# A strip of zeros of 320 numbers in place of 448 behind each gather of a graph network

## What is computed

```
h = relu(layernorm(x))                       # 12500 x 128
q, k, v = h @ Wq.T, h @ Wk.T, h @ Wv.T       # 8 heads of 16
s  = (q[dst] * k[src]).sum / 4 + edge_attr @ We.T
a  = exp(s - segment_max(s, dst)) / segment_sum(...)
x  = x + segment_sum(v[src] * a, dst)
h  = relu(layernorm(x))
for W, b, g, beta in three layers:           # relu in the first two
    h = segment_sum((h @ W)[src] * norm, dst) + b
    h = batch_norm(h) * g + beta
out = x + h
```

## Time and profile before

| | us |
|---|---|
| median of three runs | 6214.33 |
| the profiled execution, its time | 6205.67 |
| the profiled execution, its span | 6203.9 |
| PE busy in the span | 5259.4 (85%) |
| DVE busy | 4526.3 (73%) |
| POOL busy | 4496.4 (72%) |
| ACT busy | 2295.7 (37%) |
| attend, from to | 220 to 2749 |
| aggregate, layers 1, 2, 3, from to (rounded) | 3550 to 4290, 4470 to 5230, 5400 to 6120 |

### The profile page before, as it was taken

One profiled execution on the slowest core, in us unless ns is written; L12 is line 12 of the kernel. 1 busy time (PEld: TensorE's weight loads), 2 busy tenths in 40 slices (PEclk: granted clock), 3 DMA queues, 4 the chain that ended last, 5 costly groups with the idle time before them and its releaser, 6 DMA issues. The chain is left out here.

```text
span 6203.9 us, 165021 instructions
## 1 busy us (share of the span) xinstructions
PE 5259.4 (85%) x49582; PEld 3541.0 (57%) x49582; DVE 4526.3 (73%) x13500; ACT 2295.7 (37%) x5686; POOL 4496.4 (72%) x6062
## 2 busy tenths in 40 slices
PE   3688888888888888874799699998899997699995
PEld 2355555555555555553577467675476765467674
DVE  7566666666666666668899688886488887788886
ACT  3333333333333333333344244443644443444442
POOL 2588888888888888867000198886298886588883
PEclk9655565555555655555677699999999999899997
DMA  4433333333333333324333443333433334533335
GB/s 134 137 100 99 100 99 99 99 99 100 99 98 100 99 99 99 99 80 134 110 92 95 122 117 112 112 117 99 136 113 114 114 112 106 179 112 114 114 111 163
DMA packets 542000, 688.39 MB, mean 111 GB/s; under 512 B 217072, under 2 KB 427905, under 8 KB 541722
## 3 DMA queue, kind: packets, MB, share of 16 engines
q0 software_dynamic: 140208, 338.71, 19.8%
q1 hardware_dynamic: 401692, 348.45, 18.8%
HBM read 619.25 MB, written 67.52 MB: 111 GB/s over the span
## 5 line engine op out<-in xcount | busy, mean ns | idle before, releaser
L730 POOL DMA_INDIRECT at_kv<-kv_tab,at_idx x1568 | 1541.5, 983 | 276.6 <-POOL at_rest L734 139.6
L2247 ACT ACTIVATE ag_msg<-ag_pair 128x768 bf16<-128x768 f32 x1200 | 944.2, 809 | 1371.1 <-PE ag_pair L2177 1298.5
L2186 PE MATMUL ag_sum<-ag_hot,ag_msg 128*128 128x240 bf16 x10800 | 1267.4, 267 | 1.1 <-DVE ag_msg L2116 0.7
L2186 PEld LDWEIGHTS ag_sum<-ag_hot,ag_msg 128*128 128x128 bf16 x10800 | 982.9, 98 | 334.0 <-issue 287.6
L2058 POOL DMA_INDIRECT ag_spill<-g_tab,ag_idx x600 | 587.2, 979 | 687.0 <-DMA ag_idx<-spill_tab 578.5
L2099 DVE TENSOR_SCALAR ag_hot<-iota_win,ag_node 128x240 bf16<-128x240 bf16 x4350 | 994.4, 339 | 0.0
L2067 POOL DMA_INDIRECT ag_spill<-g_tab,ag_idx x750 | 731.1, 975 | 126.3 <-POOL ag_rest L2070 80.9
L2177 PE MATMUL ag_pair<-xs,ag_pick 128*32 128x384 bf16 x14400 | 758.9, 330 | 67.3 <-issue 62.9
L734 POOL MEMSET at_rest<- 8x448 f32 x1568 | 723.2, 461 | 0.1
L2116 DVE CAST ag_msg<-ag_pair 128x768 bf16<-128x768 f32 x600 | 570.2, 950 | 131.5 <-PE ag_pair L2177 104.8
L2177 PEld LDWEIGHTS ag_pair<-xs,ag_pick 128*32 128x32 bf16 x14400 | 301.0, 96 | 330.0 <-issue 214.7
(11 more groups left out here) (333 smaller groups left out, 9313.9 us busy)
## 6 DMA issues: line engine op xcount, KB each, us to landing
ag_pick<-slot_tab SPq DMA_DIRECT2D x150, 768.0 KB
rk_hi_bc<-hi_tab SPq DMA_DIRECT2D x50, 896.0 KB
at_attr<-attr SPq DMA_DIRECT2D x196, 128.0 KB
at_qd<-q_tab SPq DMA_DIRECT2D x1568, 12.0 KB
at_kv<-kv_tab,at_idx POOLq DMA_INDIRECT x1568
ag_spill<-g_tab,ag_idx POOLq DMA_INDIRECT x1350
tr_dv<-dinv_tab SPq DMA_DIRECT2D x72, 256.0 KB
g_tab<-xs SPq DMA_DIRECT2D x48, 384.0 KB
```

Source lines behind the costliest of these rows:

```text
L730: nc.gpsimd.indirect_dma_start(kv[:, s.slot, ch, :], None, env["kv_tab"], bass.IndirectOffsetOnAxis(ap=idx[:, s.slot, ch:ch + 1], axis=0)) ...
L2186: last = nc.tensor.matmul(sum_ps[k][:, 0:WIN], row[:, part * DIM:(part + 1) * DIM], hot[:, k, ch, :], start=first and part == 0, stop=end ...
L2247: nc.scalar.activation(msg[:, p % 4, :, :], pair_ps[p % 3][:, :, 0:3 * DIM], ACT.Copy).then_inc(copied[p], 1)
```

## The change

One constant is smaller, so that each of the 1568 memsets of attend (L734) and each of the 1350 of the three aggregates (L2061, L2070) writes 8x320 numbers in place of 8x448. The instructions of every engine keep their number, their order and their waits.

```diff
-REST = 448
+REST = 320
```

## The result

In the comparison that the prediction was made for, the changed kernel took a median of 7122.66 us (four runs, 7109.76 to 7139.39) against 6213.55 of before (6210.10 to 6214.83): a ratio of 1.1468, 95% interval 1.1454 to 1.1482. Forecast were 6046 us, with a range up to 6130. The same changed kernel, run later on another chip beside the same kernel before, took 6039.44 us against 6212.68 (ratio 0.9723, interval 0.9692 to 0.9754). What stands between 7123 and 6039 is what the experiments had to find.

What follows compares the result with a forecast made beforehand. POOL was taken to bound attend and, by a little, the aggregates; savings of 118 us in attend and 50 in the aggregates gave 168, so 6038 from the profiled 6205.67, stated as 6046 us for the median, range 5985 to 6130.

Steps and rivals of the forecast that it cites:

- The memset: Strip memset after each gather in attend and the aggregates: 461 ns falls to 354 in attend, saving 107 ns each.
- clean distance: Attend: time from one gather to the next with nothing held, 1.573 us before, 1.466 us after the change.
- Attend, on a full chip: Attend, forecast for any chip: block falls from 12.91 to 12.31 us, saving 118 us over 196 blocks.
- The phase on which the forecast rests: Attend: L808 runs about 9.9 us after the last gather, so one gather start per block falls inside it.
- The held gathers: Attend: gathers starting within L808 are held, 0.45 us per block, mean of L730 rising from 983 to some 1010 ns.
- Rival A: Attend: nothing held more than now, the full 0.856 us per block saved, total 5996 us; chance 0.13.
- rival B: Attend: one gather per block held the full 1.08 us, only the aggregates' 50 us remain, 6164 us; chance 0.13.
- The wait of L767 for `at_kv`: Attend: DVE's wait for gathered rows before its product should shrink from 218.5 to some 100 us.
- The aggregates, on a full chip: Aggregates, forecast for any chip: POOL's gathers drop to 13.97 us, PE sets the round, saving 50 us, range 35 to 71.
- PE's own round: Aggregates: time between two L2217 with no idle time before the second, 14.49 us, taken as the new bound.
- DVE's own round: Attend: DVE's block without its wait for gathered rows, 12.91 less 1.11, taken as 11.80 us.
- Rival C: Attend: held time spreads to DVE's small two-input instructions, block 13.94 us, total 6366 us, slower; chance 0.07.

Runs made afterwards that it cites:

- e9: The changed kernel word for word, run again beside the kernel before on a chip with nearly complete semaphore-update records; 6039.44 us, ratio 0.9723.
- e11: The kernel before, unchanged, profiled on the same chip as e9; 6214.81 us.
- e8: Kernel before with the 320 strip in attend and no gathers from attend's fifth block on, rows of the first four reused; 5816.60 us.
- e16: The kernel of e8 once more, on a thin chip (many semaphore-update records missing); 5907.05 us, kernel before there 6308.11.
- e6: Kernel before, strip 448, with the eighth gather and its memset left out from attend's fifth block on; 5932.11 us.
- e12: The kernel of e6 once more, on a chip called thin by its records alone; 5943.81 us, kernel before there 6204.42.
- e5: Kernel before with only the memsets shortened to 320 in all stages, the tile staying at 448 so addresses stay; 6032.94 us.
- e1: Kernel before with the 320 strip in attend only, 448 in the aggregates; 6736.29 us, kernel before there 6305.62.
- e4: Kernel before with strip 256 in all stages; 7769.40 us, kernel before there 6305.62.
- e2: Kernel before with the 320 strip in the three aggregates only, 448 in attend; 7033.03 us, kernel before there 6305.62.
- e3: Kernel before with strip 384 in all stages; 7100.05 us, kernel before there 6305.62.
- e15: Kernel before with strip 320 in attend and, from the fifth block on, gathers fetching a quarter of the bytes in as many rows; thin chip, 6778.95 us.
- e14: Kernel before with strip 320 in attend and two more memsets per block to slow POOL again; thin chip, 6590.15 us, kernel before there 6201.17.

## Why the prediction was wrong, step by step

**The memset.** Forecast 354 ns and a clean distance of 1.466 us; measured 355 ns in after and 354 in e9, and 1.47 between gathers. Right.

**Attend, on a full chip.** The phase on which the forecast rests is there: from the last gather of a block to L808 are 9.9 us at the median, in e9 as in e11. Forecast 12.31 us per block and 118 us; e9 against e11 gives (2662.1 - 248.8) / 195 = 12.38 and (2768.8 - 250.7) / 195 = 12.91, that is 105 us. The ends of these sums are in the rows of L808 of e9 and e11:

```profile
L808 DVE TENSOR_TENSOR at_msg<-at_kv,at_msg x196: 1210/1219/1270, 248.8 to 2662.1; 128x1024 f32<-128x1024 f32 x196
```
```profile
L808 DVE TENSOR_TENSOR at_msg<-at_kv,at_msg x196: 1210/1218/1270, 250.7 to 2768.8; 128x1024 f32<-128x1024 f32 x196
```

**The held gathers.** Forecast a mean of 1010 ns for L730, 0.45 us held per block. The page of e9:

```profile
L730 POOL DMA_INDIRECT at_kv<-kv_tab,at_idx x1568 | 1602.9, 1022 | 277.6 <-POOL at_rest L734 188.5
```

That is 8 x 0.070 = 0.56 us, 0.11 more than forecast, and this term is what makes the block 12.38 and not 12.31. A smaller error of the sum: of the 0.33 us by which the block before is longer than the clean one it names 0.13 and 0.25, which are 0.38, so that the same terms counted on both sides would have saved 0.65 us per block and not 0.60. Rival A (nothing held any more than before) would have had 983 ns or less, and rival B some 1090. By the Trainium skill's page Perfetto Trace Analysis, section DMA Instruction — SWDGE (GPSIMD), such instructions do not read a tensor, by which none would be held at all; the traces do not agree, with a longest gather of 2.02 us in e9. The wait of L767 for `at_kv` fell from 229.4 us in e11 to 163.1 in e9, where I had said some 100.

**The aggregates, on a full chip.** Forecast 50 us. First to last L2217: 2547.1 us in e11 (3558.6 to 6105.7) and 2486.2 in e9 (3454.7 to 5940.9), 61 us. The spans of PE are 14.6 us, and its own round was put at 14.49. POOL waits for PE before L2067 now (24.1 us in e9), as forecast. The spans of the whole program, 6213.1 and 6045.0 us, differ by 168.1; the sum was 168. That it comes out to the microsecond is luck: attend gave 13 us less than forecast and the aggregates 11 more.

**The step that failed** is the one that no rival took up: "PE's own round is what lies between two L2217", and "DVE's own round would be about 1.1 us shorter". Both were taken as constants of the kernel. On a thin chip they are not: there PE's results come the later, and these rounds are the longer, the closer POOL's gathers stand. With them 1.47 us apart PE's results come 3 us late, DVE's round is 15.06 us instead of at most 11.80, and PE's in the aggregates over 18 instead of 14.49. The prediction said that it would fail "if PE's round in aggregate rises above 14.49", which it did, but it gave that no chance and no price. Rival C had the right sign with the wrong mechanism: it had gathers held by DVE, and in after hardly any is (mean 960 ns, where 952 is a gather that is not held).

**DVE's own round** was also too long in itself. Without gathers it is 10.90 us (e8) and 10.83 (e16), not 11.80: the 1.11 us of waiting for `at_kv` are not all that the gathers cost. With seven of the eight gathers the whole block is 11.50 (e6). Part of this may be PE's clock, whose granted value in attend (250 to 2200 us) is 0.68 in e8, 0.64 in e6 and 0.58 in before. The sum did not rest on it.

**Could the trace of before have told?** It had two signs. The landing times were missing from its list of DMA issues (though e12 shows that a thin trace can have them), and in 100 of the 196 blocks DVE's wait before L786 was put down to "issue", where e11 names PE nearly always:

```profile
DVE at_ml L786 <- issue: 111.3, 100, 1.4
```

Of e11, the same line of the waits:

```profile
DVE at_ml L786 <- issue: 4.2, 4, 1.1
```

Neither gives a price, and one trace alone doesn't show that they are unusual.

## What to carry to other kernels

A strip that keeps two indirect DMAs apart may protect something that waits for nobody in the profile: before it is cut, look for instructions that start well after the recorded end of what they wait for ("remote" or "issue" before an instruction with a clear producer). If the engine that was sped up then waits for the rest, ask what the others do slower, not what it does. And a result that can't be understood is first to be had again on another chip, with the kernel before beside it, ahead of any theory: here e5 alone would have seemed to prove a theory of addresses that is false.

## What the runs showed of the hardware

**Two kinds of chip for one program.** Before takes 6200 to 6218 us in six of the eight comparisons, thin or full, and 6306 and 6308 in two thin ones. The changed kernel takes 7123 us where it was first compared and 6039 on a full chip; the same short strip in another tile takes 7135 on a thin one and 6033 and 6038 on full ones. The seven comparisons of the experiments were on seven chips, each given once, so it is open whether the kind belongs to the chip, to its state at that time or to the way in which that execution was recorded.

**Gathers against PE.** On thin chips, by the distance of gathers; e1 to e4 are from one chip, on which before takes 6306 us:

| strip | distance, us | block of attend, us | span of aggregate, us |
|---|---|---|---|
| no gathers | | 10.83 (e16) | |
| 448 | 1.573 | 12.95 (e2), 12.91 (before) | 15.5 (e1), 14.97 (before) |
| 384 | 1.52 | 15.12 (e3) | 18.1 (e3) |
| 320 | 1.47 | 15.24 (e1), 15.06 (after) | 20.5 (e2), 18.4 (after) |
| 256 | 1.41 | 15.72 (e4) | 21.8 (e4) |

The distances are those of attend. In the aggregates the memsets are longer (405 ns in the mean in after, 511 in before) and neighbouring gathers stand 1.62 us apart at the median with 448, 1.57 with 384, 1.51 with 320 (after) and 1.42 with 256.

In attend the step lies between 1.52 and 1.57 us. In the aggregates it isn't as sharp: on the two chips on which before takes 6306 and 6308 us, 448 gives 15.5 (e1) and 15.7 us (e15, e16), and 14.97 on the first one. The number of gathers per block is not what counts (e14); whether it is the mean distance of neighbours or the shortest is open. DVE's and ACT's results are not late; only PE's are.

**A possible cause, argued and not shown.** The thin traces lack more than a third of the records of semaphore updates (e16, with no gathers in attend, a fifth), and the late engine is the one with most instructions, 49582 matmuls and as many weight loads of 165021. A single path for records that is slower on thin chips and holds up its busiest producer would explain both, and also that a quarter of the bytes changes nothing. The Trainium skill, NOTIFIC — the notification-queue block, section Overflow: three behaviours, one of which stalls the engine, says that the block's internal pipeline always holds back its producers rather than lose a record inside. No run here shows this block at work, or whether an execution that is not recorded would be late too. By the Trainium skill, SBUF — State Buffer, section Who interferes with whom, PE shares no port with anyone and DMA never contends with a compute engine; e15, where a quarter of the data leaves the delay as it was, agrees that it isn't the bytes that land in SBUF.
